# Graph attention and routed mixtures, two rounds: softmax with one exponential a graph, row sums on ScalarE, and small operations of the second pass moved from GpSimd to VectorE

## What is computed

```
x = x + elu(attention(layernorm(x), adj, W0, a0))        leaky slope 0.2
x = x + mixture0(layernorm(x))      8 experts, the best 2 of a node, gelu
x = x + relu(attention(layernorm(x), adj, W1, a1))       leaky slope 0.01
x = x + mixture1(layernorm(x))      32 experts, the best 1 of a node, relu

attention(x):  h = x W
               e[i, j] = leaky_relu(h[i] . a1 + h[j] . a2)
               softmax of e over the j that adj allows, times h
```

## Time and profile before

| | |
|---|---|
| median of 3 runs | 1112.64 us (1110.25 to 1114.04) |
| the profiled execution | 1112.51 us, span 1110.8 us |
| TensorE busy | 888.1 us (80%), mean granted clock 0.879 |
| VectorE busy | 788.0 us (71%) |
| GpSimd busy | 765.7 us (69%) |
| ScalarE busy | 699.1 us (63%) |
| GpSimd scatters L505 | 256, 258.8 us, 1011 ns each |
| exponentials L1121, L1122 | 256 each, 103.1 and 104.8 us |
| maxima and sums L718 | 256, 61.8 us, 288 ns each |
| maximum of the scores L745 | 64, 43.8 us, 685 ns each |

### The profile page before, as it was taken

How to read it: one execution, slowest core, us unless ns; L and a number is a source line. 1 busy time by engine, 2 the same in 40 slices (tenths; PEclk the granted TensorE clock), 3 DMA queues, 4 the chain that set the end, 5 groups by cost and what they waited for, 6 DMA issues and landing times. The chain is left out here.

```text
span 1110.8 us, 26952 instructions
## 1 busy us (share of the span) xinstructions
PE 888.1 (80%) x6709; PEld 799.2 (72%) x6709; DVE 788.0 (71%) x3507; ACT 699.1 (63%) x2364; POOL 765.7 (69%) x983
## 2 busy tenths in 40 slices
PE   5988898888619999999999669999999418888720
PEld 4777787777509999999999658888888406666620
DVE  7688989898848999999999617888888713322310
ACT  3998988898405655656656369999998216643300
POOL 4347767777753888887788801778787846777776
PEclk9998989898659999999999979999999659976655
DMA  9333442221167888877878221222221135433301
GB/s 213 69 96 118 135 133 60 64 73 33 40 141 201 210 212 211 206 210 209 207 206 208 66 68 39 79 79 79 79 81 51 53 96 145 116 99 105 93 31 38
DMA packets 144904, 129.21 MB, mean 116 GB/s; under 512 B 26521, under 2 KB 116510, under 8 KB 144754
## 3 DMA queue, kind: packets, MB, share of 16 engines
q1 hardware_dynamic: 124114, 91.94, 33.4%
q0 software_dynamic: 17760, 34.20, 9.1%
q10 hardware_dynamic: 2880, 1.35, 0.6%
HBM read 82.74 MB, written 47.48 MB: 117 GB/s over the span
## 5 line engine op out<-in xcount | busy, mean ns | idle before, releaser
L505 POOL DMA_INDIRECT xs<-staged,dst x256 | 258.8, 1011 | 77.0 <-issue 68.5
L1172 ACT ACTIVATE hT<-bank,wt 128x128 f32<-128x128 f32 x620 | 177.3, 368 | 131.3 <-PE bank L1392 115.3
L551 POOL DMA_INDIRECT x2d<-ob,xi x155 | 161.3, 1040 | 41.6 <-issue 27.3
L573 POOL DMA_INDIRECT out<-oq,xq x144 | 142.8, 991 | 58.2 <-issue 42.7
L1378 PE MATMUL bank<-xnT,wt 128*128 128x128 f32 x1240 | 165.8, 277 | 0.0
L1392 PE MATMUL bank<-w2s,hT 128*128 x1240 | 164.1, 275 | 0.6 <-DVE ob L1044 0.5
L1378 PEld LDWEIGHTS bank<-xnT,wt 128*128 128x128 f32 x1240 | 152.6, 194 | 0.1
L1392 PEld LDWEIGHTS bank<-w2s,hT 128*128 128x128 f32 x1240 | 150.9, 192 | 1.0 <-issue 1.0
L1121 ACT ACTIVATE p<-bank,nm 128x128 f32<-128x128 f32 x256 | 103.1, 403 | 19.6 <-DVE nm L746 19.6
L1122 ACT ACTIVATE p<-bank,nm 128x128 f32<-128x128 f32 x256 | 104.8, 410 | 0.0
L1135 ACT ACTIVATE rl<-bank,rinv 128x128 f32<-128x128 f32 x256 | 97.1, 453 | 3.1 <-DVE staged L738 3.1
(11 more groups left out here) (249 smaller groups left out, 2202.6 us busy)
## 6 DMA issues: line engine op xcount, KB each, us to landing
wt<-wpd SPq DMA_DIRECT2D x155, 258.0 KB
xi<-xs SPq DMA_DIRECT2D x155, 66.0 KB
xq<-xs SPq DMA_DIRECT2D x144, 66.0 KB
xb<-x2d SPq DMA_DIRECT2D x32, 258.0 KB, 3.2
xb<-in_x SPq DMA_DIRECT2D x32, 256.0 KB, 3.2
wpd<-w1c SPq DMA_DIRECT2D x56, 129.0 KB, 3.3
xs<-staged,dst POOLq DMA_INDIRECT x256, 2.6
x2d<-ob,xi POOLq DMA_INDIRECT x155
```

The costliest lines, as they stand in the source:

```text
L505: pool.indirect_dma_start(out=xs[l], out_offset=bass.IndirectOffsetOnAxis(ap=dst[b % ND][:, c:c + 1], axis=0), in_=stag[s][:, q, 0:ROW], i ...
L551: pool.indirect_dma_start(out=x2d, out_offset=bass.IndirectOffsetOnAxis(ap=xi[t % NXI][:, ID:ID + 1].bitcast(U32), axis=0), in_=ob[:, t % ...
L573: pool.indirect_dma_start(out=orow, out_offset=bass.IndirectOffsetOnAxis(ap=xq[j % NXQ][:, q, ID:ID + 1].bitcast(U32), axis=0), in_=oq[j % ...
L1172: last = act.activation(hT[t % 2][:, j, :], HID[t % 2][:, j, :], ACT.Gelu, bias=wt[t % NW][:, c:c + 1])
```

## The change

In both passes the leaky score itself is computed, once, into a tile `leaky` in SBUF: s plus its negative part times (slope - 1). In the first pass ScalarE computes the negative part (a Relu of (slope - 1) x s, counted by `below`), between its copy `x1T` and `xs_`; in the second VectorE does, with a tensor_scalar. VectorE adds s (counted by `leaky`) and takes the negative maximum of the result as `nm`. ScalarE then computes one exponential a graph from SBUF, straight into `pm`, with the row sums through its accumulator. The L718 are gone, and the layer norm's small operations stand in front of the wait for the exponentials. `leaky`, `nm`, `pm` and `rsum` have two buffers. TensorE may write a bank of scores again after VectorE's addition, and transposes `pm` after the exponentials. In the second pass VectorE also adds the constant to the variance (into `ve1`) and writes the token numbers (from a table `tcol4` of four columns); GpSimd only takes the power. The first pass keeps GpSimd's addition and iota.

```diff
@@ allocations
+        tcol4 = sb("tcol4", [P, G])
+        ve1 = sb("ve1", [P, G])
-        nm = sb("nm", [P, G])
-        p1 = sb("p1", [P, G, P])
-        p2 = sb("p2", [P, G, P])
-        pm = sb("pm", [P, G, P])
+        nm = [sb(f"nm{s}", [P, G]) for s in range(2)]
+        leaky = [sb(f"leaky{s}", [P, G, P]) for s in range(2)]
+        pm = [sb(f"pm{s}", [P, G, P]) for s in range(2)]
-        rsum = sb("rsum", [P, G])
+        rsum = [sb(f"rsum{s}", [P, G]) for s in range(2)]
@@ GpSimd, spreads
-                e = eps[:, h, own] if l == 0 else eps1[:, :]
-                v = var[:, own] if l == 0 else mv[:, :, 1]
-                pool.tensor_tensor(ve[:, own], v, e, ALU.add).then_inc(sem("var_eps"), 1)
+                if l == 1:
+                    pool.tensor_tensor(stag[s][:, :, RS], ve1[:, :], neghalf[:, 0:G], ALU.pow).then_inc(sem("rstd"), 1)
+                    return
+                pool.tensor_tensor(ve[:, own], var[:, own], eps[:, h, own], ALU.add).then_inc(sem("var_eps"), 1)
@@ VectorE, stats1
-                after(dve, "var_eps", m + APART - 1)
                 for q in range(G):
                     last = dve.bn_aggr(mv[:, q, :], st[:, q, :])
-                last.then_inc(sem("moments"), 1)
+                mark(last)
+                dve.tensor_scalar(stag[m % NS][:, :, ID].bitcast(I32), tcol4[:, :], float(T * (m - NG)), None,
+                                  ALU.add).then_inc(sem("ids"), 1)
+                after(dve, "rstd", m + APART - 1)
+                settled()
+                dve.tensor_scalar(ve1[:, :], mv[:, :, 1], EPS, None, ALU.add).then_inc(sem("moments"), 1)
@@ VectorE, weights
+                for part in moments:
+                    part()
                 after(dve, "exps", n)
-                after(dve, "pt_ps", n - 1)
                 after(dve, "er", n - 3)
-                for q in range(G):
-                    last = dve.scalar_tensor_tensor(pm[:, q, :], p1[:, q, :], 0.0, p2[:, q, :], ALU.max, ALU.max,
-                                                    accum_out=rsum[:, q:q + 1])
-                    if q == 3:
-                        last.then_inc(sem("pm"), 1)
-                    if q % 2 and moments:
-                        moments[q // 2]()
-                after(dve, "pm", n)
-                dve.reciprocal(rinv[n % 3][:, :], rsum[:, :]).then_inc(sem("rinv"), 1)
+                dve.reciprocal(rinv[n % 3][:, :], rsum[n % 2][:, :]).then_inc(sem("rinv"), 1)
@@ VectorE, scores
-                after(dve, "s_ps", n)
-                after(dve, "exps", n - 1)
-                link(dve.reduce_max(nmax[:, :], g4(SB[n % 2]), AX.X, negate=True))
-                dve.scalar_tensor_tensor(nm[:, :], nmax[:, :], SLOPE[l], nmax[:, :], ALU.mult, ALU.min).then_inc(sem("nm"), 1)
+                S, L = g4(SB[n % 2]), leaky[n % 2][:, :, :]
+                if l == 0:
+                    after(dve, "below", n)
+                else:
+                    after(dve, "s_ps", n)
+                    after(dve, "exps", n - 2)
+                    link(dve.tensor_scalar(L, S, 0.0, SLOPE[l] - 1.0, ALU.min, ALU.mult))
+                dve.tensor_tensor(L, L, S, ALU.add).then_inc(sem("leaky"), 1)
+                after(dve, "leaky", n)
+                dve.reduce_max(nm[n % 2][:, :], L, AX.X, negate=True).then_inc(sem("nm"), 1)
@@ ScalarE, graph_layer
                         after(act, "nm", m)
-                        after(act, "pm", m - 1)
-                        S = g4(SB[m % 2])
+                        after(act, "pt_ps", m - 2)
+                        after(act, "rinv", m - 2)
                         for q in range(G):
-                            act.activation(p1[:, q, :], S[:, q, :], ACT.Exp, bias=nm[:, q:q + 1])
-                            last = act.activation(p2[:, q, :], S[:, q, :], ACT.Exp, bias=nm[:, q:q + 1], scale=SLOPE[l])
+                            last = act.activation(pm[m % 2][:, q, :], leaky[m % 2][:, q, :], ACT.Exp, bias=nm[m % 2][:, q:q + 1],
+                                                  accum_out=rsum[m % 2][:, q:q + 1])
...
+                    if l == 0 and 0 <= i - 1 < NG:
+                        m = n - 1
+                        after(act, "s_ps", m)
+                        after(act, "exps", m - 2)
+                        act.activation(leaky[m % 2][:, :, :], g4(SB[m % 2]), ACT.Relu, scale=SLOPE[l] - 1.0).then_inc(sem("below"), 1)
@@ TensorE, graph_layer
-                        after(pe, "exps", m - 2)
+                        after(pe, "leaky", m - 2)
...
-                        after(pe, "pm", n - 2)
+                        after(pe, "exps", n - 2)
...
-                        turn(XP, pm, "pt_ps")
+                        turn(XP, pm[n % 2], "pt_ps")
```

More of the change, by code:

```diff
@@ L124, in program @@
         eps = sb("eps", [P, 2, 2 * G])
-        eps1 = sb("eps1", [P, G])
         powers = sb("powers", [P, E0])
@@ L155, in program @@
         iota = sb("iota", [P, E1 + 1])
-        tcoli = sb("tcoli", [P, 2], I32)
-        tcol = sb("tcol", [P, 2])
+        tcoli = sb("tcoli", [P, G], I32)
+        tcol4 = sb("tcol4", [P, G])
+        tcol = tcol4[:, 0:2]
         regi = [sb(f"regi{l}", [P, E1 // 2], I32) for l in range(2)]
@@ L435, in _ @@
                 pool.memset(eps[:, h, h * G:(h + 1) * G], EPS)
-                pool.memset(eps[:, h, (1 - h) * G:(2 - h) * G], EPS * EPS / (1.0 + EPS))
-            pool.memset(eps1[:, :], EPS).then_inc(sem("eps"), 1)
+                last = pool.memset(eps[:, h, (1 - h) * G:(2 - h) * G], EPS * EPS / (1.0 + EPS))
+            last.then_inc(sem("eps"), 1)
             def spreads(l, i):
@@ L484, in _ @@
             pool.iota(iotai[:, :], pattern=[[1, E1 + 1]], base=0, channel_multiplier=0)
-            pool.iota(tcoli[:, :], pattern=[[P, 2]], base=0, channel_multiplier=1)
+            pool.iota(tcoli[:, :], pattern=[[P, G]], base=0, channel_multiplier=1)
             for l in range(2):
@@ L683, in numbers_ready @@
                 dve.tensor_copy(iota[:, :], iotai[:, :])
-                dve.tensor_copy(tcol[:, :], tcoli[:, :])
+                dve.tensor_copy(tcol4[:, :], tcoli[:, :])
                 for l in range(2):
```

## The result

The changed kernel takes **1134.81 us** (median of 4 runs, 1130.17 to 1137.70) against 1112.16 for the kernel before beside it (4 runs): ratio 1.0194, 95% interval 1.0166 to 1.0222, 22.7 us slower. The forecast was 7 us slower; the result lies above its range.

The account below looks back on a forecast made before the run. No engine is free in either pass; loops of waits among VectorE, TensorE and ScalarE set the pairs. First pass plus 7.5, second pass's first steps plus 1.0, end minus 1.4: plus 7.1, so 1119.6 us, range 1114 to 1126.

Parts of the forecast that it names:

- First steps without routing: First pass before routing: ScalarE's work grows by 0.48 us and shrinks by 0.7, so nothing is added.
- Clean pair 16.0: First pass, two steps in which nothing holds VectorE up: 16.0 us against 15.6, plus 0.4.
- Slow pairs 18.8: First pass, pairs with TensorE's clock at 0.50 and late scores: 18.8 us against 18.11, plus 0.7.
- sum plus 7.5: First pass: three clean pairs at 0.4 and nine slow ones at 0.7 add 7.5 us.
- A row sum 0.08 us: ScalarE's exponentials: each row sum adds 0.08 us, so four graphs cost 1.3 us, from 2.0 before.
- Second pass 13.63 a pair: Second pass: pairs take 13.63 us against 13.62, so nothing is gained.
- First steps plus 1.0: Second pass before routing: one or two steps of 5.7 us become 6.38, plus 1.0.
- End -1.4: End of second pass, GpSimd working alone: four spreads at 0.36 us saved each, minus 1.4.
- (c): First pass: every pair becomes slow, adding 23.6 us, sum 1135.7; chance 0.11.
- (a): First pass: slow clock spells go, 1101.8 us if no pair is slow, 1110 if half go; chance 0.24.
- (b): Second pass is bound by GpSimd: 32 steps at 0.36 us give -11.5, so 1108.5; chance 0.11.
- (d): Exponentials not halved, a row sum costs 0.25 us: second pass waits 0.3 us a pair, 1123; chance 0.06.

Follow-up runs that it names:

- run 1: The changed kernel with ScalarE's Relu of the first pass placed behind xs_ instead of in front of it: 1138.29 us, ratio 1.0192 to the kernel before.
- run 5: The changed kernel with VectorE computing the negative part of groups 0 to 6, ScalarE's Relu only that of groups 7 to 31: 1123.87 us.
- run 7: The changed kernel with four unread products on TensorE ahead of its x1 wait, in first-pass routing steps and steps 4 to 7: 1111.13 us.
- run 6: The kernel before with four unread products on TensorE ahead of its x1 wait in the first pass's routing steps: 1099.78 us, ratio 0.9871.
- run 3: The change in the second pass alone, first pass as in the kernel before: 1116.33 us, ratio 1.0005 to the kernel before.
- run 8: The kernel before with only the second pass's constant and token numbers moved from GpSimd to VectorE, exponentials unchanged: 1115.94 us, ratio 1.0015.
- run 13: The changed kernel with 76 unread products on TensorE behind the second pass: 1130.43 us, ratio 1.0159 to the kernel before.

## Why the prediction was wrong

- **First steps without routing: "nothing". This step failed.** It counted ScalarE's work (plus 0.48, less 0.7) and not its order. The prediction had the fact, "behind this wait stand xs_, hg, pt and xT on ScalarE", and priced it in the pairs alone. Measured: 13.6 us. The order closed two loops. Steps 2 to 4 cost 7.3 us, 5.9 of them steps 2 and 3, the first loop's; steps 5 to 7, the second loop's, cost 5.1, of which 3.5 were clock; 1.2 came before the first maximum (runs 1, 5, 7).
- **Clean pair 16.0**: 15.92, and 15.98 as the mean at full clock. Right. VectorE waited 0.43 us for the Relu, forecast 0.65.
- **Slow pairs 18.8, sum plus 7.5**: plus 8.1. The total is right, its make-up is not: eleven pairs were slow, not nine, at 16.7 to 18.8 us, so the agreement is in part luck. At full clock 2.8 of it are left, the rest was the clock (runs 6, 7).
- **A row sum 0.08 us**: 0.13 (below), so 1.5 us a group and not 1.3. It was not on the path: VectorE's reciprocal waited 1.2 us in all for it between 40 and 300 us.
- **Second pass 13.63 a pair**: 13.66, right, and the reason too (runs 3, 8). First steps plus 1.0: no loss, -0.3 in all. End -1.4: -2.1.
- **The second mixture** had no term: plus 6.7 in the profiled execution, about 4 in the medians, the clock (run 13).
- **Rivals.** (c), 1135.7 us, is nearest in number by luck: its price, 18.83 us for every pair, did not come: 17.54. Two terms it did not have, first steps and second mixture, make up the sum. (a) came only with the fill. (b) falls by run 8. (d) falls: an exponential with its row sum takes 0.38 us, two without took 0.50.

## What to carry to other kernels

Before an instruction with a wait is put into an engine's program, follow what stands behind it round to what it waits for, once for each kind of step: where the path closes, the step is as long as the loop, however idle the engines are. Moving the instruction can open one loop and lengthen another, as in run 1. Price a kernel whose TensorE clock falls to half in short waits by two numbers, clean and slow, and test early whether cheap unread products in that wait hold the clock; here they gave 1.3% in the kernel before and took the changed one from 1.9% slower to 0.3% faster. Work taken from an engine that already waits comes back as waiting.

## What the runs showed of the hardware

ScalarE in order of time, the changed kernel; each exponential with a row sum is two instructions:

```profile
24.30 0.39 ACT L1125 ACTIVATE pm<-leaky,nm 128x128 f32<-128x128 f32 x1
24.59 0.19 ACT L1125 ACTIVATION_READ_ACCUMULATOR pm<-leaky,nm 128x1 f32 x1
24.68 0.39 ACT L1125 ACTIVATE pm<-leaky,nm 128x128 f32<-128x128 f32 x1
```

They start 0.38 us apart where the earlier trace rows had 0.25: a row sum of 128 elements costs ScalarE 0.13 us; VectorE's reading of its own takes 0.08. And the same idle stretch of 1.41 us ahead of x1's transposes stands before full speed in the earlier trace rows (four transposes in 0.66 us) and before half speed at 205.87 us in the changed kernel (1.12 us for the same four): its length alone does not say which.
